# Moving the softmax normalisation of three head groups of the first attention from DVE to Pool

## The reference

```python
qh = (q @ Wq.T + bq)...; kh = (k @ Wk.T + bk)...; vh = (v @ Wv.T + bv)...   # q = layernorm(x), k = v = ctx
attn = einsum('bhqd,bhkd->bhqk', qh, kh) * scale
attn = softmax(where(mask, -inf, attn))
out = einsum('bhqk,bhkd->bhqd', attn, vh)
x = x + (out @ Wo.T + bo)
```

## Time and profile before

| what | value |
|---|---|
| median of 3 runs | 1827.51 us (1823.39 to 1827.77) |
| the profiled execution: time, span | 1828.99 us, 1827.3 us |
| busy over the span: PE, DVE, ACT, Pool | 1501.3, 903.3, 496.4, 451.6 us |
| first attention | from the start to about 480 us |
| its reciprocals on DVE | 16 of 3.36 us |

### The profile page before, as it was taken

One profiled execution on the slowest core, in us unless ns is written; L12 is line 12 of the kernel. 1 busy time (PEld: TensorE's weight loads), 2 busy tenths in 40 slices (PEclk: granted clock), 3 DMA queues, 4 the chain that ended last, 5 costly groups with the idle time before them and its releaser, 6 DMA issues. The chain is left out here.

```text
span 1827.3 us, 19385 instructions
## 1 busy us (share of the span) xinstructions
PE 1501.3 (82%) x6088; PEld 889.5 (49%) x6088; DVE 903.3 (49%) x1684; ACT 496.4 (27%) x620; POOL 451.6 (25%) x261
## 2 busy tenths in 40 slices
PE   5888888889619999922599989998899979996996
PEld 2334343343518777721345445444544454435785
DVE  5566566656410000012357654776366635656566
ACT  2433324325102222200033322333133313330221
POOL 2000000000130000041034442445144514471333
PEclk8899899999759999966699989999899989996998
DMA  6523113220253544225556634555256625502001
GB/s 158 143 35 39 26 17 46 35 36 1 87 210 121 181 154 164 110 79 79 72 72 81 92 46 62 76 81 69 35 73 94 83 35 73 69 1 95 1 1 46
DMA packets 62234, 136.08 MB, mean 74 GB/s; under 512 B 10592, under 2 KB 21216, under 8 KB 57568
## 3 DMA queue, kind: packets, MB, share of 16 engines
q1 hardware_dynamic: 59440, 127.26, 37.1%
q0 software_dynamic: 2736, 8.13, 1.3%
HBM read 58.55 MB, written 12.06 MB: 39 GB/s over the span
## 5 line engine op out<-in xcount | busy, mean ns | idle before, releaser
L1260 POOL TENSOR_TENSOR a_probs<-a_probs 128x1024 f32<-128x1024 f32 x128 | 305.1, 2384 | 476.7 <-PE a_p_o L1594 475.7
L1299 ACT ACTIVATE a_probs<-a_p_s 128x1024 f32<-128x1024 f32 x160 | 163.9, 1024 | 332.0 <-PE a_p_s L1580 331.9
L417 DVE CUSTOM_DVE_ANT_0 a_scratch<-a_p_m,a_bias_q 128x512 bf16<-128x512 f32 x256 | 163.8, 687 | 121.0 <-PE a_p_m L572 121.0
L1402 DVE TENSOR_REDUCE a_max_ctx<-a_p_m 128x1 f32<-128x512 f32 x256 | 169.3, 688 | 77.0 <-PE a_p_m L1555 73.7
L327 ACT ACTIVATE a_probs<-a_p_s 128x1024 f32<-128x1024 f32 x128 | 130.7, 1025 | 178.8 <-PE a_p_s L597 178.3
L595 PE MATMUL a_p_s<-a_q_stack,a_k_stack 128*128 128x512 f32 x256 | 121.7, 502 | 31.2 <-DMA a_q_stack<-a_neg_max 31.2
L572 PE MATMUL a_p_m<-a_k_stack,a_q_stack 127*128 127x512 f32 x256 | 130.4, 555 | 13.9 <-DVE a_mx L417 7.0
L1594 PE MATMUL a_p_o<-a_probs,a_v 128*64 128x512 f32 x512 | 138.7, 620 | 0.0
L1014 PE MATMUL e_p_h<-e_rows_t,e_w 128*128 128x256 f32 x480 | 123.1, 390 | 13.8 <-DVE e_rows_t L952 13.8
L1426 DVE RECIPROCAL a_recip<-a_p_sum 128x512 f32<-128x512 f32 x32 | 106.9, 3339 | 29.3 <-PE a_p_sum L1605 29.3
L1023 PE MATMUL e_p_y<-e_w,e_hidden 128*128 128x256 f32 x480 | 118.6, 380 | 0.6 <-ACT e_hidden L868 0.6
(11 more groups left out here) (198 smaller groups left out, 2183.9 us busy)
## 6 DMA issues: line engine op xcount, KB each, us to landing
e_w<-in_L_w SPq DMA_DIRECT2D x30, 1024.0 KB, 8.2
a_q_hh<-a_hi SPq DMA_DIRECT2D x64, 256.0 KB, 5.5
a_q_lm<-a_lo SPq DMA_DIRECT2D x32, 256.0 KB, 6.9
a_k_hl<-a_hi SPq DMA_DIRECT2D x32, 256.0 KB, 7.7
a_k_hl<-a_lo SPq DMA_DIRECT2D x32, 256.0 KB, 9.1
a_k_h<-a_hi SPq DMA_DIRECT2D x32, 256.0 KB, 10.3
a_ctx_t<-in_ctx_t SPq DMA_DIRECT2D x8, 512.0 KB, 5.7
a_q_stack<-a_hi SPq DMA_DIRECT2D x32, 128.0 KB, 5.6
```

The costliest lines, as they stand in the source:

```text
L417: dve.tensor_tensor_reduce(scratch[:, fill.n % M_BANKS, :], m, bias_q[:, i % NT, :], 1.0, -3.0e38, ALU.add, ALU.max, mx[:, i:i + 1]).then_ ...
L1260: pool.tensor_tensor(probs[:, kt], probs[:, kt - 1], probs[:, kt], ALU.add)\
L1299: act.activation(probs[:, kt, :, :], p_s[:, (KT1 * p + kt) % 2, :, :], ACT.Exp).then_inc(exp_done.sem, 1)
L1402: dve.tensor_reduce(max_ctx[:, NT * head + t:NT * head + t + 1], m, AX, ALU.max)\
```

## The change

For groups 0 to 2 DVE now only copies the spread sums out of PSUM into SBUF (`bring_sums`). Pool raises them to the power of minus one, in place, against one column of -1.0 that is broadcast, and multiplies `o_norm[:, g]` by the result (`divide`). Two semaphores count this: `inverted` (the power) and `divided` (the product). Since there is one buffer `sums`, DVE may copy the next group's sums only when Pool has divided the group before. The last group stays on DVE (`normalize_last`), into the same buffer, so its reciprocal waits for Pool's third product as well.

```diff
-        norm_ready = Count(sem("norm_ready"), NG0)
+        norm_ready = Count(sem("norm_ready"), 1)
+        inverted = Count(sem("inverted"), NG0 - 1)
+        divided = Count(sem("divided"), NG0 - 1)
...
+            def divide(b, ahead):
+                freed = 0
+                for g in range(NG0):
+                    for j in range(PARTS):
+                        for what in steps(g, j, ahead):
+                            freed += DVE_FILLS.get(what, 0)
+                            if what == "sums":
+                                m_free.wait(pool, b, freed)
+                                pool.tensor_tensor(sums[:], sums[:], minus_one[:].broadcast_to([P, S]), ALU.pow)\
+                                    .then_inc(inverted.sem, 1)
+                                inverted.wait(pool, b, g)
+                                pool.tensor_tensor(o_norm[:, g - 1, :], o_norm[:, g - 1, :], sums[:], ALU.mult)\
+                                    .then_inc(divided.sem, 1)
...
-            def normalize(b, fill, freed, g):
+            def bring_sums(b, fill, g):
                 m = fill.bank()
                 if g:
-                    norm_ready.wait(dve, b, g)
+                    divided.wait(dve, b, g)
                 m_full.wait(dve, b, fill.n)
-                dve.reciprocal(recip[:], m).then_inc(m_free.sem, 1)
+                dve.tensor_copy(sums[:], m).then_inc(m_free.sem, 1)
+
+            def normalize_last(b, fill, freed):
+                m = fill.bank()
+                divided.wait(dve, b, NG0 - 1)
+                m_full.wait(dve, b, fill.n)
+                dve.reciprocal(sums[:], m).then_inc(m_free.sem, 1)
                 m_free.wait(dve, b, freed)
-                dve.tensor_tensor(o_norm[:, g, :], o_norm[:, g, :], recip[:], ALU.mult).then_inc(norm_ready.sem, 1)
+                dve.tensor_tensor(o_norm[:, NG0 - 1, :], o_norm[:, NG0 - 1, :], sums[:], ALU.mult)\
+                   .then_inc(norm_ready.sem, 1)
```

More of the change, by code:

```diff
@@ L115, in attention0 @@
         minus_half = sb("minus_half", [P, NT])
+        minus_one = sb("minus_one", [P, 1])
         zero = sb("zero", [P, H0])
@@ L126, in attention0 @@
         neg_max = sb("neg_max", [G0 * NT, P], F32R)
-        recip = sb("recip", [P, S])
+        sums = sb("sums", [P, S])
         o_norm = sb("o_norm", [P, NG0, S])
@@ L271, in _ @@
             pool.memset(minus_half[:], -0.5)
+            pool.memset(minus_one[:], -1.0)
             pool.memset(ident[:], 0.0)
@@ L300, in _ @@
                 bias(b)
+                divide(b, True)
+            divide(B - 1, False)
         @block.scalar
@@ L352, in turn @@
                 read_output(b, NG0 - 1)
-                norm_ready.wait(act, b, NG0)
+                divided.wait(act, b, NG0 - 1)
+                norm_ready.wait(act, b, 1)
             fill = Fill(m_full.per - BEFORE + NT)
@@ L452, in turn @@
                             elif what == "sums":
-                                normalize(b, fill, freed, g - 1)
+                                bring_sums(b, fill, g - 1)
                             elif what in FILLS:
@@ L461, in turn @@
                         begin_norm(b)
-                normalize(b, fill, freed + 1, NG0 - 1)
+                normalize_last(b, fill, freed + 1)
                 if ahead:
@@ L647, in turn @@
                     if i == 0:
-                        norm_ready.wait(pe, b, NG0)
+                        divided.wait(pe, b, NG0 - 1)
+                        norm_ready.wait(pe, b, 1)
                     for k in range(2):
```

## The result

The changed kernel takes 2633.81 us (median of 4 runs, 2632.94 to 2636.73), the kernel before 1826.61 us (4 runs). The span went from 1827.3 to 2633.0 us.

What follows compares the result with a forecast made beforehand. PE was taken as the fullest engine in every stretch of the first attention. Rounds in series +1079.5, gain at the rows -8.7 and low clock +8.8 made +1079.6 us on the median 1827.51: 2907 us, range 1840 to 3070.

Steps and rivals of the forecast that it cites:

- The rounds in series: First attention: three rounds of copy, power and product per batch, 107.2 us each, run one after another, +1079.5 us in all.
- The power: Pool's power over 512 columns in groups 0 to 2: 105 us each, the middle of 95 and 115 us.
- by the column: Likeliest case: Pool's power pays for each column, 90 to 118 us; 2730 to 3065 us in all, chance 0.60.
- between: Rival: columns overlap on Pool, so a power takes 6.4 to 90 us; 1833 to 2730 us, chance 0.22.
- The cheap rival: Pool's power takes 2.2 us, its rounds are hidden, only the 8.7 us gain is left: 1818.8 us, chance 0.10.
- the fixed-part reading: Lower end for Pool's power: all 1.02 us at four columns is fixed, further columns run at the addition's rate, 2.2 us.
- The copy (0.69) and the product (1.25): Each round: DVE's 128x512 copy from PSUM takes 0.69 us, Pool's product on half of 1024 columns 1.25 us.
- The gain at the rows: End of group 1, three batches with `rows`: bank free earlier, transposes' 2.09 us wait gone, 2.9 us each, -8.7 us.
- The cap by the maxima's DMA: Group 1's end: the score can come no sooner than 6.71 us after the DMA's issue, limiting the gain to 2.96 us.
- The low clock after the stalls: End of each batch: PE starts at the lower clock after the long stall, 2.2 us each, +8.8 us.
- Groups 1 and 2 give nothing: The copies at groups 2 and 3 gain nothing, since PE waits there for the maxima's DMA and for ACT.

Runs made afterwards that it cites:

- one group: Kernel before with only group 0 divided by Pool, groups 1 to 3 staying on DVE with a buffer of their own: 1946.14 us, ratio 1.0649.
- three buffers: Changed kernel with three buffers for the sums in place of one: 2610.75 us, ratio 1.4285 to the kernel before.
- the list of prices: Kernel before with Pool powers and products of several sizes added behind its last bias addition, where Pool is idle: 1829.82 us, one run.
- the cheap product: Changed kernel with Pool's power replaced by a product with minus one, sums of groups 0 to 2 not inverted: 1809.43 us, ratio 0.9896.

## Why the prediction was right, and where it was off

The forecast was 2907 us in a range of 1840 to 3070; measured were 2633.81. The mechanism was right and one term was mis-sized. The range was wide enough to hold almost any price of the power; the likeliest case's own range, 2730 to 3065, missed the result.

- **The rounds in series.** Right. With the power as measured, a round by the prediction's parts is 0.69 + 0.09 + 81.92 + 0.1 + 1.26 + 0.03 = 84.09 us; it was 84.15. Twelve of them less 206.5 make 803, of 805.7 measured. The experiments with one group and with three buffers came out about 1 us from what this chain gives (1946.14 for 1945, 2610.75 for 2611).
- **The power.** Right in kind (by the column), wrong in size: 105 us forecast, 81.92 measured. The step that failed is the fixed part. I bounded it by other calls of Pool, 0.124 and 0.284 us; it is 0.39 us. A tenth of a microsecond beyond the upper bound, divided by four columns and multiplied by 512, is 13 us a power, and from the middle value it is 23. Twelve powers make -277 us, which is the whole miss of 273. I also called the case "by the column" 90 to 118 us long and so gave its chance to a stretch that didn't hold the value; 82 us lay in what I had called "between". DVE's waits, forecast at some 80, 80 and 100 us, were 62.0, 68.9 and 83.5, and the first attention ended at 1287 us in place of 1560, both for the same reason. The cheap rival, which the fixed-part reading would have given, is shown false by the list of prices. The Trainium skill (GPSIMD Engine Reference, Elementwise, side-by-side cycle accounting) gives 2.6 cycles per element for two inputs. The products here are near it: 256 more columns cost 0.53 us (0.73 to 1.26), 2.1 ns each, which is an estimated 2.5 cycles at that section's 1.2 GHz. The power does not follow it, with 159 ns a column.
- **The copy (0.69) and the product (1.25).** Measured 0.691 and 1.26 us.
- **The gain at the rows, -8.7 us.** Wrong place. It lies between the copies of groups 0 and 1, that is inside the first round, where DVE then waited 62.03 us; it was hidden. My own sum had the rounds in series and took it off all the same. Its size, 2.9 us, was off as well: the score came 4.03 us after the copy began (94.79 in the changed kernel's trace) where it had come 8.01 us after the reciprocal began, 3.98 us earlier, and 4.54 for the whole stretch with the cheap product. The cap by the maxima's DMA was wrong, since I carried 6.71 us over from group 2. The trace of the kernel before has both landings: the DMA (8 KB) landed 2.8 us after its issue in group 1 and 6.6 us in group 2. In the changed kernel it landed after 1.8 us in group 1, and the score came 5.68 us after the issue (89.11 to 94.79), behind the projection and without a wait for it. So the score was not released by the DMA, as I had forecast. Without the cap the prediction's own terms were near: the projection started 2.85 us earlier (2.5 forecast) and took 1.98 us in place of 3.53 (up to 1.65 less forecast). In group 2 the DMA engines were busy with the stacks, in group 1 they were idle, as the DMA share of the two stretches in the kernel before shows (the next to last column). That this is what delays the landing fits the rows, and no run isolates it:

```profile
89.99:96.70 6.71, 3.86 (x22) 1.61 (x14) 5.02 (x6) 1.58 (x2) 0.00 (x0) 1.00 0.02 5
118.33:125.04 6.71, 2.54 (x14) 0.80 (x7) 4.05 (x2) 1.26 (x2) 0.00 (x0) 0.98 0.63 69
```

- **The low clock after the stalls, +8.8 us.** Near at the stall itself and too large in the sum. From group 3's reciprocal to the first addition of the output projection it was 10.22, 10.34 and 10.38 us in place of 8.09, 8.08 and 8.07: 2.1 to 2.3 us for each, where I had 2.2. The rest of the way to the next copy was then 0.4, 0.5 and 1.0 us shorter than before, for a reason that no run shows, so that +4.8 is left of three times 2.2. In the last batch the 2.2 us did not come at all: 14.05 us in place of 15.55. Those -1.5 us are not the stall's either, since with the cheap product, without any stall, it is 14.05 as well.
- **The sum of the two small terms.** They were -8.7 and +8.8 and cancelled each other. Measured, everything outside the three rounds adds up to +2.6 us. That the two errors nearly cancelled was luck; either alone would have been under 9 us.
- **Groups 1 and 2 give nothing.** Right: in the first batch 23.34 and 5.01 us with the cheap product against 23.38 and 5.01.

The output projection of the first batch shows the clock after the stall in its rows, first in the changed kernel (a window that ends after eleven matmuls), then in the kernel before:

```profile
347.35 4.84 PE L681 MATMUL a_p_m<-a_wo,a_o_norm 128*128 128x256 f32 x11 [83.94 <-DVE a_o_norm L462]
152.60 7.14 PE L652 MATMUL a_p_m<-a_wo,a_o_norm 128*128 128x256 f32 x32 [0.82 <-DVE a_o_norm L435]
```

Eleven matmuls took 0.44 us each, where 32 took 0.22 each in the kernel before. The granted clock in the stretch before it was 0.52, near the level of 1.2 GHz.

## What to carry to other kernels

A price that the trace knows at one size only has two unknowns, and the fixed part that one assumes is multiplied by the ratio of the sizes: measure the operation at two sizes in an idle place of the kernel before moving it. When an engine waits for a reader to free a bank, first try a cheap copy out of the bank on the same engine and the slow work behind what is urgent; here that gave about 13 us with no second engine, where the hand-over cost 807. And before taking a gain off a sum, ask whether it lies inside a stretch that the sum already counts as hidden.

## What the hardware did that I had not expected

- A power on Pool costs 0.16 us for each column plus 0.34 to 0.39 us (1.02 us at 4, 41.23 at 256, 81.92 at 512 columns), and as much on 32 partitions as on 128 (10.53 and 10.55 us at 64 columns).
- Twelve powers over real sums took 81,915 to 81,937 ns each, and those over the constant 37.0 lie on the same line, so nothing in them hints at a dependence on the values.
- DVE's reciprocal of 128x512 takes nearly as long from SBUF (3.34 us) as from PSUM (3.36 us).
- An 8 KB DMA landed 2.8 us after its issue at a DMA share of 0.02 and 6.6 us after it at a share of 0.63.
